# Attention scores of two graph layers issued together in four row groups, the second layer's mask moved from TensorE to VectorE, and new hand-written engine orders

## What the reference computes

```
layer 0: q,k,v = x@W + b, 8 heads of 32 features; scores = q k^T per head,
         scores = where(adj == 0, -16384, scores); pros = softmax(scores)
         z = v; four times: z = 0.9 * pros @ z + 0.1 * v;  x = layernorm(x + z)
layer 1: one head over 256 features, masked softmax, x = layernorm(x + w V Wo + bo)
layer 2: 8 heads of 32 features, scores = where(adj == 0, -inf, q k^T / sqrt(32)),
         softmax, h = attn v, x = layernorm(x + h Wo + bo)
layer 3: four label masks (adj == 1..4), per label a mean over neighbours, a linear
         layer, then a gated unit (r, z, n) and a layernorm
```

## Time and profile before

| | |
|---|---|
| time, median of 3 runs | 1781.53 us (1780.1 to 1781.58) |
| time of the profiled execution | 1783.61 us |
| span of the profiled execution, first to last instruction | 1781.8 us |
| granted TensorE clock, mean over the span | 0.987 |
| PE busy | 1728.4 us (97%) |
| ACT busy | 1190.9 us (67%) |
| DVE busy | 1102.2 us (62%) |
| POOL busy | 793.9 us (45%) |
| DMA | 28 GB/s on average |

### The profile page before, as it was taken

The page is one execution under the profiler, slowest core; times in us unless marked ns, Lnnn a source line. Parts: engine busy times, 40 slices in busy tenths (PEclk is TensorE's granted clock), DMA queues, the critical chain, the costliest instruction groups (busy, mean ns, idle before and its releaser), DMA issues.

```text
span 1781.8 us, 48249 instructions
## 1 busy us (share of the span) xinstructions
PE 1728.4 (97%) x17680; PEld 1549.8 (87%) x17680; DVE 1102.2 (62%) x2741; ACT 1190.9 (67%) x4008; POOL 793.9 (45%) x774
## 2 busy tenths in 40 slices
PE   5799999999999999999999999999999999999995
PEld 4688899998899998899998899998899998889885
DVE  3665666665666665666665666665666666666662
ACT  4576777666777666776666776666777666677652
POOL 1354444444444444444444544444544454544441
PEclk8999999999999999999999999999999999999998
DMA  5000011000000000001001011000011000000000
GB/s 182 27 22 25 20 31 31 17 27 29 18 29 29 20 22 29 18 29 29 23 18 29 18 29 29 27 14 29 18 29 29 29 12 29 19 28 21 13 16 13
DMA packets 70982, 49.39 MB, mean 28 GB/s; under 512 B 4368, under 2 KB 69904, under 8 KB 70288
## 3 DMA queue, kind: packets, MB, share of 16 engines
q1 hardware_dynamic: 70928, 48.66, 9.1%
HBM read 40.26 MB, written 8.39 MB: 27 GB/s over the span
## 4 chain that ended last, share of the span: by engine, by line
PE 93%; issue 2%; DVE 2%; ACT 2%; POOL 1%; DMA 0%; SPq 0%; POOLq 0%; DVEq 0%
PE bank_A L375 15%; PE bank_B L375 10%; PE bank_A L409 7%; PE bank_A L602 6%; PE bank_A L424 5%; PE bank_B L593 5%; PE bank_A L593 5%; PE bank_B L424 4%; PE bank_C L418 3%; PE bank_X L387 3%; PE bank_X L375 3%; PE bank_C L375 3%; PE bank_B L387 2%; PE bank_X L520 2%; PE bank_A L563 2%
## 5 line engine op out<-in xcount | busy, mean ns | idle before, releaser
L802 POOL TENSOR_TENSOR E<-E,rsum 128x512 f32<-128x512 f32 x256 | 266.4, 1041 | 565.3 <-DVE rsum L898 420.2
L810 POOL TENSOR_TENSOR rstd<-var,minus_half 128x2 f32<-128x2 f32 x128 | 92.4, 722 | 283.2 <-DVE var L933 277.4
L409 PEld LDWEIGHTS bank_A<-kT,qT 32*128 32x128 f32 x1024 | 123.2, 186 | 36.4 <-issue 27.1
L680 ACT ACTIVATE vnat<-bank_A 128x256 f32<-128x256 f32 x96 | 36.9, 384 | 170.0 <-PE bank_A L486 169.9
L375 PE MATMUL bank_A<-xT_hi,w_hi 128*128 128x256 f32 x512 | 138.8, 294 | 11.6 <-DVE xT_lo L869 11.6
L409 PE MATMUL bank_A<-kT,qT 32*128 32x128 f32 x1024 | 147.6, 283 | 0.5 <-ACT E L669 0.5
L409 PE MATMUL bank_B<-kT,qT 32*128 32x128 f32 x1024 | 147.6, 283 | 0.0
L375 PE MATMUL bank_A<-xT_hi,w_lo 128*128 128x256 f32 x512 | 132.3, 281 | 0.0
L834 POOL TENSOR_TENSOR E<-E,rcnt 128x512 f32<-128x512 f32 x64 | 78.3, 1245 | 113.7 <-DVE rcnt L1005 113.7
L693 ACT ACTIVATE xT_hi<-bank_A,col 128x256 fp32r<-128x256 f32 x128 | 65.3, 562 | 94.5 <-PE bank_A L393 94.5
L409 PEld LDWEIGHTS bank_B<-kT,qT 32*128 32x128 f32 x1024 | 123.2, 186 | 0.0
(11 more groups left out here) (198 smaller groups left out, 6143.9 us busy)
## 6 DMA issues: line engine op xcount, KB each, us to landing
adj<-in_adj SPq DMA_DIRECT2D x96, 128.0 KB, 2.4
xt_in<-in_xt SPq DMA_DIRECT2D x64, 128.0 KB, 2.2
x_in<-in_x SPq DMA_DIRECT2D x32, 256.0 KB, 2.7
out<-out_sb SPq DMA_DIRECT2D x32, 256.0 KB, 2.2
absent<-in_adj SPq DMA_DIRECT2D x32, 128.0 KB, 2.1
stage<-in_weights SPq DMA_DIRECT2D x3, 1024.0 KB, 10.7
row<-in_rows SPq DMA_DIRECT2D x1, 1152.0 KB, 10.1
stage<-in_l_weights SPq DMA_DIRECT2D x1, 1024.0 KB, 7.5
```

Of the source, the lines that this page charges most:

```text
L409: mm = nc.tensor.matmul(b[:, at:at + P], qT[hs, c, ns], kT[hs, c, ns], start=masked_by is None, stop=masked_by is None or (g, c) == (G - 1 ...
L802: nc.gpsimd.tensor_tensor(e, e, rs[:, part].unsqueeze(2).to_broadcast([P, SB, P]), ALU.mult).then_inc(e_sig.sem, 1)
L810: nc.gpsimd.tensor_tensor(rstd[part][:], var[part][:], minus_half[:], ALU.pow)\
```

## The change

- The steps `s0` and `s2` become one step `s02`, in two halves. Its half `part` issues, in turn, matmuls of layer 0 of iteration `it` into banks A0, B0 and of layer 2 of iteration `it - 2` (APART) into banks A2, B2. Layer 0 takes heads 0, 1 and then 2, 3 of each group of four; layer 2 takes 2, 3 and then 0, 1 (HEADS2), so that four matmuls in a row lie in four different row groups and four banks. The step exists for 34 iterations instead of 32, and in the first two and the last two holds one layer alone. It waits for what both layers' halves waited for.
- The mask matmuls of layer 2 (L401) and the POOL step `ne2` go. POOL makes a second 0/1 mask (`absent.2`), and DVE gets four predicated copies per period for layer 2 (`fill2.x`), each ahead of its `max2.x`.
- The reload of layer 2's adjacency waits for the last `fill2` instead of `ne2`; the last group of weights is loaded within SP's list instead of ahead of it.
- All five order tables are new.

```diff
@@ ORDER, tensor: before, then after
-        "ni@4 z@4 k0 q0 v0 s0.0 l1w n1@1 k2@2 wt.0@3 mixt@4 q2@2 vb0 v2@2 g1@1 s0.1 p0.0 n3@3 s2.0@2 vo1@1 wt.1@3",
-        "p0.1 lab.0@3 lab.1@3 s1@1 lab.2@3 lab.3@3 p0.2 s2.1@2 p0.3 out@3 hop0.0 hop0.1 p1@1 p2.0@2 back0.0 back0.1",
-        "p2.1@2 nh@3 hop0.2 hop0.3 o1@1 back0.2 back0.3 p2.2@2 p2.3@2 hop0.4 hop0.5 rh@3 hop2.0@2 back0.4 back0.5",
-        "hop2.1@2 ri@3 hop0.6 hop0.7 wo2.0@2 back0.6 wo2.1@2 n2@1 back0.7",
+        "p2.2@3 p1@2 back0.2@1 p2.3@3 back0.3@1 o1@2 n3@4 hop0.4@1 hop0.5@1 hop2.0@3 hop2.1@3 back0.4@1 wo2.0@3",
+        "back0.5@1 wt.1@4 hop0.6@1 hop0.7@1 wo2.1@3 back0.6@1 lab.0@4 n2@2 lab.1@4 back0.7@1 k0 lab.2@4 q0 k2@2 q2@2",
+        "v2@2 n1@1 lab.3@4 s02.0 v0 out@4 nh@4 vb0 l1w rh@4 g1@1 ri@4 s02.1 p0.0 ni@4 p0.1 z@4 p0.2 vo1@1 p0.3 wt.0@3",
+        "s1@1 hop0.0 hop0.1 mixt@4 p2.0@2 back0.0 back0.1 p2.1@2 hop0.2 hop0.3",
@@ ORDER, scalar (after)
+        "out@5 exp2.0@3 exp2.1@3 exp0.1@1 l1w@1 split.1@1 vb0@1 nh@5 r@5 x0 p0.0@1 g1@2 exp0.2@1 p0.1@1 exp0.3@1 n@5",
+        "p0.2@1 z@5 vo1@2 p0.3@1 split.2@1 exp2.2@3 exp2.3@3 exp1@2 back0.0@1 back0.1@1 split.3@1 p2.0@3 p2.1@3 p1@2",
+        "back0.2@1 p2.2@3 p2.3@3 back0.3@1 hi3@4 t3@4 wt.0@4 back0.4@1 back0.5@1 split.4@1 wt.1@4 lab.0@4 hi2@2 t2@2",
+        "k0 q0 lab.1@4 lab.2@4 k2@2 q2@2 hi1@1 lab.3@4 t1@1 v0 exp0.0",
@@ ORDER, gpsimd (after)
+        "sc.3@5 pow.0@1 absent.0 absent.2@2 sc.0@1 sc.1@2 sh.1@2 e0.0 e0.1 wm@3 e2.0@2 e0.2 e0.3 sh.3@5 pow.2@3",
+        "e2.1@2 e2.2@2 e2.3@2 e1@1 pow.3@4 sh.0@1 pow.1@1 ne1",
@@ ORDER, vector (after)
+        "rec2.2@3 hop0.1@1 bn.3@5 rec2.3@3 rec1@2 hop0.2@1 agg.3@5 eps.3@5 hop0.3@1 nrm.3@5 x0 y1@2 hop0.4@1 hop2.0@3",
+        "hop0.5@1 split.2@1 hop2.1@3 bn.1@2 lo3@4 agg.1@2 eps.1@2 y2.0@3 hop0.6@1 hop0.7@1 nrm.1@2 y0.0@1 y2.1@3",
+        "y0.1@1 split.3@1 lo2@2 bn.0@1 mask@3 agg.0@1 eps.0@1 split.4@1 bn.2@3 nrm.0@1 v2@2 cnt@3 fill0.0 max0.0",
+        "fill2.0@2 guard@3 max2.0@2 fill2.1@2 max2.1@2 fill0.1 rcnt@3 lo1@1 o_hi@4 max0.1 l1w rec0.0 o_lo@4 rec2.0@2",
+        "agg.2@3 rec0.1 fill0.2 max0.2 gate@4 fill0.3 max0.3 rows split.1 rec0.2 fill2.2@2 sum@4 rec2.1@2 max2.2@2",
+        "rec0.3 fill2.3@2 mixa@4 eps.2@3 max2.3@2 mixb@4 mixc@4 nrm.2@3 max1@1 hop0.0",
@@ TensorE, scores
-            def scores(banks, qT, kT, pair, masked_by=None):
-
-                if masked_by is not None:
-                    for b in banks:
-                        nc.tensor.matmul(b[:, :], ident_b[:], masked_by[:].unsqueeze(2).to_broadcast([P, G, NC, P]),
-                                         start=True, stop=False)
+            def scores(runs):
+
                 for g in range(G):
                     for c in range(NC):
                         at, ns = (g * NC + c) * P, slice(g * P, (g + 1) * P)
-                        for j, b in enumerate(banks):
-                            h = 2 * pair + j
-                            hs = slice(h * HD, (h + 1) * HD)
-                            mm = nc.tensor.matmul(b[:, at:at + P], qT[hs, c, ns], kT[hs, c, ns],
-                                                  start=masked_by is None,
-                                                  stop=masked_by is None or (g, c) == (G - 1, NC - 1))
+                        for banks, qT, kT, heads in runs:
+                            for b, h in zip(banks, heads):
+                                hs = slice(h * HD, (h + 1) * HD)
+                                mm = nc.tensor.matmul(b[:, at:at + P], qT[hs, c, ns], kT[hs, c, ns],
+                                                      start=True, stop=True)
                 return mm
@@ TensorE, the step
+                if step == "s02":
+                    runs, ready = [], []
+                    if exists(it):
+                        if part == 0:
+                            wait(pe, k0_ready, it, 1)
+                            wait(pe, q0_ready, it, 1)
+                        else:
+                            wait(pe, exp0, it, 2)
+                        runs.append((AB0, qT0, kT0, (2 * part, 2 * part + 1)))
+                    it2 = it - APART
+                    if exists(it2):
+                        if part == 0:
+                            wait(pe, q2_ready, it2, 1)
+                            wait(pe, v2_ready, it2, 1)
+                        else:
+                            wait(pe, exp2, it2, 2)
+                        runs.append((AB2, qT2, kT2, HEADS2[2 * part:2 * part + 2]))
+                    scores(runs).then_inc(s02_ready.sem, 1)
@@ VectorE
+                if step in ("fill0", "fill2"):
...
+                    nc.vector.copy_predicated(s, m, f).then_inc((filled0 if L == 0 else filled2).sem, 1)
```

More of the change, by code:

```diff
@@ L88, in table @@
     return steps
-LAST_LAG = max(lag for engine in ORDER for _, _, lag in table(engine))
+APART = 2
+EXTRA = {"s02": APART}
+HEADS2 = [2, 3, 0, 1]
+LAST_LAG = max(lag + EXTRA.get(step, 0) for engine in ORDER for step, _, lag in table(engine))
 def periods(eng, engine):
@@ L103, in periods, with exists @@
             for step, part, lag in steps:
-                if 0 <= n - lag < ROUNDS:
+                if 0 <= n - lag < ROUNDS + EXTRA.get(step, 0):
                     yield step, part, n - lag
+def exists(it):
+    return not isinstance(it, int) or 0 <= it < ROUNDS
 def starts(it):
@@ L160, in gnn_program @@
         row = sb("row", [P, len(ROWS), D])
-        fill = sb("fill", [P, 1])
+        fill = sb("fill", [P, 2])
         minus_half = sb("minus_half", [P, G])
@@ L351, in _ @@
                 if step == "ld_adj" and not starts(it):
[L352 to L355, removed]
+                    if part in (0, 2):
+                        wait_before(sp, filled0 if part == 0 else filled2, it, HC)
                     else:
-                        wait_before(sp, masked, it, 1)
+                        wait_before(sp, ne1_ready if part == 1 else masked, it, 1)
                     load_adj(part, it)
+                if step == "ldw" and starts(it):
+                    sp.wait_ge(w_split, SPLIT["2"])
+                    load_weights(4)
                 if step == "store":
@@ L419, in transpose_heads, with attend @@
                 return mm
-            def attend(bank, vnat, PT, g):
+            def attend(bank, vnat, PT, g, order=range(HC)):
                 for h in range(HEADS):
@@ L424, in attend @@
                     mm = nc.tensor.matmul(bank[hh * HD:(hh + 1) * HD, c * P:(c + 1) * P],
-                                          vnat[:, g, h * HD:(h + 1) * HD], PT[:, hh, g, c], start=True, stop=True)
+                                          vnat[:, g, h * HD:(h + 1) * HD], PT[:, order.index(hh), g, c],
+                                          start=True, stop=True)
                 return mm
@@ L460, in _ @@
                     mm.then_inc(v0_back.sem, 1)
-                if step == "s0":
-                    if part == 0:
-                        wait(pe, k0_ready, it, 1)
-                        wait(pe, q0_ready, it, 1)
-                    else:
-                        wait(pe, exp0, it, 2)
-                    scores(AB0, qT0, kT0, part).then_inc(s0_ready.sem, 1)
+                if step == "s02":
[16 more added lines that the diff above has]
+                    scores(runs).then_inc(s02_ready.sem, 1)
                 if step == "p0":
@@ L541, in _ @@
                     natural(B2, "v2", xT_hi[2], xT_lo[2]).then_inc(proj2.sem, 1)
-                if step == "s2":
-                    if part == 0:
-                        wait(pe, q2_ready, it, 1)
-                        wait(pe, v2_ready, it, 1)
-                        wait(pe, ne2_ready, it, 1)
-                    else:
-                        wait(pe, exp2, it, 2)
-                    scores(AB2, qT2, kT2, part, no_edge2).then_inc(s2_ready.sem, 1)
                 if step == "p2":
@@ L558, in _ @@
                     wait(pe, pt2_ready, it, 4)
-                    attend(AB2[part], vnat2, PT2, part).then_inc(o2.sem, 1)
+                    attend(AB2[part], vnat2, PT2, part, HEADS2).then_inc(o2.sem, 1)
                 if step == "wo2":
@@ L850, in split_lo @@
                                         group(w_hi, j).bitcast(F32), ALU.subtract).then_inc(w_split, 1)
-            nc.vector.memset(fill[:], -16384.0)
+            nc.vector.memset(fill[:, 0:1], -16384.0)
+            nc.vector.memset(fill[:, 1:2], -3e38)
             nc.vector.memset(minus_half[:], -0.5)
@@ L968, in _ @@
                 if step == "max2":
-                    if part % 2 == 0:
-                        wait(dve, s2_ready, it, part // 2 + 1)
+                    wait(dve, filled2, it, part + 1)
                     nc.vector.tensor_reduce(nmax2[:, part], AB2[part % 2][:, :].rearrange("p (a n) -> p a n", a=SB),
```

57 lines of the change are left out of this document (24 added, 33 removed), and 10 rows, old and new, of the table ORDER.

## The result

The changed kernel takes 1785.49 us (median, 1783.75 to 1787.98 over 11 runs) beside 1781.06 us (1780.08 to 1783.08, 11 runs) for the one before: ratio 1.0025 [1.0016, 1.0033]. It is slower by a quarter of a per cent, where I had forecast 1687 us and put 0.93 on faster. The profiled execution has a span of 1782.0 us.

What follows compares the result with a forecast made beforehand. TensorE, busy throughout the middle, was taken as the bound. 1781.8 - 99.0 (scores) - 13.4 (attend order) + 8 (stalls) + 10 (ends) = 1687.4 us, predicted as 1687, range 1664 to 1715.

Steps and rivals of the forecast that it cites:

- Four row groups at once: TensorE's scores: four matmuls start together every 0.11 us, a combined half costs 1.18 us; saves 3.24 us a period, net 99.0.
- port conflict: Rival on TensorE's scores: row groups get in each other's way, four every 0.143 us; adds 18 us, 1705; chance 0.08.
- pairs: Rival on TensorE's scores: only two matmuls proceed at a time; adds 56 us, 1743; chance 0.07.
- The 18 us: TensorE's scores: extra time if four row groups give 3.07 times the speed, not 4; not taken into the forecast.
- The order of attend: TensorE's attend step: four separate runs instead of six, 0.21 us saved for each run less, 13.4 us in all.
- s02.1 waits for the last exponential: Rival: TensorE's second scores half waits on ScalarE's exponentials; slower than before, 1815 with a 4.5 us stall; chance 0.05.
- The steady stalls: TensorE's waits for other engines in the middle: 0.3 us a period, 8 us in all; bounds 0 and 2 us a period.
- p0.2 as tight: TensorE's p0.2 waits for GpSimd's e0.2, behind two or three multiplications of 1.04 us; within 0.5 us of being late.
- the other engines don't keep up: Rival: s02.1, p1 or p0.2 wait 1 to 2 us each period; 1707 to 1737; chance 0.08.
- The mask at nothing: VectorE's four layer 2 fills, 3.0 us a period, hidden behind TensorE's work; 96 us if nothing hid them.
- GpSimd at nothing, with 25 of 50 us used: GpSimd swaps one mask for another and has half its period spare: no cost.
- The ends: Pipeline fill and drain: layer 3 half a period later, three or four more waits, 10 us; bounds 0 and 20.

Runs made afterwards that it cites:

- e9: Changed kernel with each fill value in its own tile, and GpSimd's sh.3 (layer 3's beta) and wm (layer 3's weight scaling) ahead of e0.0: 1725.65 us, 0.9669.
- e4: Changed kernel without the four predicated copies of layer 2, whose scores stay unmasked: 1767.48 us, 0.9920.
- e1: Changed kernel with the two fill values in two one-column tiles instead of two columns of one tile: 1768.68 us, 0.9924.
- e12: e9 with projection n1 behind s02.0 on TensorE, and lab.3 ahead of hi1 on ScalarE: 1719.87 us, 0.9650.
- e5: Changed kernel with two fill tiles, GpSimd's wm ahead of e0.0 and its sh.3 moved later, just ahead of pow.3: 1758.43 us, 0.9865.

## Why the prediction was wrong, step by step

The forecast of the span was 1687.4 us, 32 periods of 49.93 and 89.6 us of ends. Measured: 32 x 52.52 and 101.4 us. So 83 of the missing 94.6 us are the period and 12 the ends. Of the 2.59 us per period, 1.97 are waits (2.27 for 0.3) and 0.62 TensorE's list (50.25 for 49.63).

- *Four row groups at once*: right. 1.10 us a half for 1.18 forecast. Over one period of e9, summing from each matmul's start to the next one's, scores and mask went from 5.41 to 2.21 us: 3.20 saved, 3.24 forecast. The rivals of a port conflict and of pairs are out. The 18 us that I had estimated from the 3.07 of the Trainium skill (TensorE: Matmul & The Clock Gate, Part 3: Packing small matmuls) don't show either: four row groups take 1.10 us where two take 1.09. No run has one row group at a time, so the figure itself isn't tested.
- *The order of attend*: half right. In the same sums attend lost 0.20 us, 0.10 for each run less and not 0.21. The rest of the list grew. In the changed kernel the label step (L600), in four runs instead of two, costs 5.96 instead of 5.74 us, the transpositions of the softmax 3.86 instead of 3.54, mixt, s1 and wt together 0.37 more; the projections take 0.28 less, out 0.18 and o1 0.10 less. All steps but scores and attend come to about 0.35 us more. I had counted the runs of the step that I looked at, and not those that the new table splits. With the 0.22 us of attend that is nearly all of the 0.62 us; why each step costs what it does in its new place isn't separated.
- *s02.1 waits for the last exponential*, the slower rival: wrong place. In the middle it never waits.
- *The steady stalls*, "Neither sets the period by its sum" and "I take 0.3 us of stall per period": this is the step that failed. The waits are 2.27 us per period, 63 us more than forecast over 32 periods. The sums were right (37.3 us of VectorE, 26.3 of GpSimd), and e4 shows that the amount isn't the bound. But I added durations as if an instruction of VectorE took the same time whatever GpSimd does. The holds of 0.7 to 1.1 us each make 1.2 us ahead of mixt and 0.9 ahead of p0.2. Even my upper bound of 2 us per period was below the 2.27, and the sum with the upper bounds of stalls and ends both is 1745 us, which my range to 1715 left out. I had named p0.2 as tight; mixt, whose three links on VectorE are all of the kind that is held, I hadn't looked at. The nearest rival was "the other engines don't keep up" with 1 to 2 us, at 0.08.
- *The mask at nothing*: right for the amount once the waits are cured (e9 has all four copies and 0.22 us of waits), not in the changed kernel, where leaving the copies out gains 18 us (e4); and wrong for the form: I priced the copies by the rows of the scalar form, and the diff of `fill` makes them another instruction. e1 puts that at 17 us.
- *GpSimd at nothing, with 25 of 50 us used*: wrong. Its busy share says nothing of what it holds up; where wm and sh.3 stand in its table decides 43 us (e1 to e9).
- *The ends*: mis-sized, 25 us for 13. In the first 220 us TensorE idles 51.2 us (220 - 168.8); the same view of the kernel before gives 32.3:

```profile
0.00:220.00 220.00, 187.72 (x1976) 162.37 (x1980) 124.21 (x298) 141.43 (x471) 86.35 (x87) 0.94 0.17 56
```

That the filling of the pipeline is longer is shown: the first mixt comes at 212.2 us instead of 181.8. That this is due to layer 3 standing half a period later is argued only, and it can hardly be all. Between the first and the fifth vb0 173.9 us pass instead of 160.8, and over these 220 us TensorE's wait ahead of the softmax's transpositions for GpSimd's products grows from 5.9 to 13.8 us, so waits for GpSimd are a part of it. The granted clock of the stretch is also lower, 0.90 instead of 0.94; what that costs isn't separated. e12 shows that the place of n1 is a small part of it. With shorter periods the ends don't shrink: in e9 they are 1723.9 - 32 x 50.30 = 114 us.

With the stalls cured (e9, e12) the same change is worth 3.3 to 3.5% instead of the forecast 5.3%, and what is left of the difference is the ends, 24 us in e9, and the 0.4 us per period of the list, 12 us.

## What to carry to other kernels

Before adding up an engine's list, look in the trace for one instruction with several durations and ask what the other engine did at its end; in these traces a running GpSimd instruction holds whatever of VectorE has two SBUF operands (1.41 to 1.60 us instead of 0.69), so the two lists have to be read side by side, not by their busy shares. When a change moves work between engines, check in the new code that the instruction is the same one that the old rows price, down to the shape of a constant's tile. And when TensorE's idle time comes back as waits of about a microsecond once per period, try the order of the engine with the most spare time first: here two words of its table took 43 us off e1. A step moved back can make another one late (e5); a step moved into idle time didn't (e9).

## What the runs showed of the hardware

- A VectorE instruction with two SBUF operands (128x512 f32, 0.69 us) waits for GpSimd's running instruction and ends 0.54 to 0.56 us after it: 0.97 us in the old kernel, 1.41 to 1.60 in the changed one. A TENSOR_SCALAR of 128x2 from SBUF to SBUF ends 0.03 us after it: 1.24 instead of 0.17. A RECIPROCAL of 128x4 from SBUF to SBUF isn't held (0.17 beside GpSimd), nor is an instruction with one of its two operands in PSUM (0.68). GpSimd is held in turn, 1.04 to 1.40 and 1.29 to 1.72 us.
- A predicated copy whose fill value is a whole tile [P, 1] runs as a scalar form, 0.75 us, and isn't held; with a column of a [P, 2] tile it runs as a two-input form, 0.69 us alone and up to 1.60 beside GpSimd.
- Four row groups writing to four banks keep the interval of two, 0.11 us; and two pairs of row groups issued one behind the other overlap at the joint (32 matmuls in 1.65 us, where the sum of two pairs one after the other gives 2.06).
